# Two attention blocks: first row maxima from the split parts in four banks, the last sums partly on TensorE, and filler matmuls at the start

## The reference

```
block 0, on x[16,128,1024]:
  h = group_norm(x, 32 groups, eps 1e-6) * scale + bias
  q, k, v = Wq^T h + bq, Wk^T h + bk, Wv^T h + bv      # 4 heads of 32 channels
  p = softmax(q^T k / sqrt(128)) over 1024 keys        # per head, 1024 x 1024
  x = (x + Wp^T (v p^T) + bp) / sqrt(2)
block 1, on that x:
  h = group_norm(x, 8 groups, eps 1e-5) * w + b
  q, k, v = qkv_w h + qkv_b                            # one head of 128 channels
  out = proj(softmax(q^T k / sqrt(128)) v) + proj_b + x
```

## Time and profile before

| what | value |
|---|---|
| time before, median of 3 runs | 1682.16 us (1681.73 to 1682.63) |
| the profiled execution's own time | 1681.49 us |
| its span in the profile | 1679.7 us |
| TensorE busy | 1604.5 us, 96% |
| VectorE busy | 1162.1 us, 69% |
| GpSimd busy | 1130.2 us, 67% |
| ScalarE busy | 1069.1 us, 64% |
| first score matmul of round 0 starts at | 66.49 us |
| last matmul of block 0's attention, then the wait for GpSimd's sums, ends at | 1596.62 us |

### The profile page before, as it was taken

One profiled execution on the slowest core, in us unless ns is written; L12 is line 12 of the kernel. 1 busy time (PEld: TensorE's weight loads), 2 busy tenths in 40 slices (PEclk: granted clock), 3 DMA queues, 4 the chain that ended last, 5 costly groups with the idle time before them and its releaser, 6 DMA issues.

```text
span 1679.7 us, 25530 instructions
## 1 busy us (share of the span) xinstructions
PE 1604.5 (96%) x9319; PEld 1067.4 (64%) x9319; DVE 1162.1 (69%) x1961; ACT 1069.1 (64%) x1825; POOL 1130.2 (67%) x535
## 2 busy tenths in 40 slices
PE   3888899999999999999999999999999999999888
PEld 2343466666666666666667666766666676766567
DVE  3677677777777777777777777677777767775342
ACT  1245576766667666766766676767667676767634
POOL 2088787676668867666786767668776766788700
PEclk8599899999999999999999999999999999999989
DMA  6132304041311404141140414113041412200000
GB/s 201 66 76 72 68 13 131 21 126 39 101 45 57 108 20 126 39 117 36 51 107 21 125 39 126 38 64 83 33 114 38 126 38 66 67 20 8 7 7 20
DMA packets 47660, 111.69 MB, mean 66 GB/s; under 512 B 5808, under 2 KB 6448, under 8 KB 47536
## 3 DMA queue, kind: packets, MB, share of 16 engines
q1 hardware_dynamic: 47536, 110.06, 23.5%
HBM read 67.84 MB, written 41.94 MB: 65 GB/s over the span
## 4 chain that ended last, share of the span: by engine, by line
PE 89%; DVE 5%; ACT 3%; DMA 2%; issue 1%; POOL 0%; SPq 0%; ACTq 0%; POOLq 0%
PE bank L899 15%; PE acc L838 14%; PE scores L877 14%; PE scores L820 14%; PE scores L864 7%; PE scores L856 4%; PE acc L904 3%; PE bank L908 3%; PE scores L857 3%; PE scores L858 3%; PE bank L904 3%; DVE halfmax L707 3%; PE bank L922 2%; PE bank L926 2%; ACT turned L569 1%
## 5 line engine op out<-in xcount | busy, mean ns | idle before, releaser
L510 POOL TENSOR_TENSOR sum<-sum,probs 128x1024 f32<-128x1024 f32 x448 | 1049.7, 2379 | 398.2 <-PE acc L838 397.0
L707 DVE TENSOR_REDUCE halfmax<-bank 128x1 f32<-128x512 f32 x1024 | 678.1, 685 | 246.3 <-PE bank L899 242.4
L549 ACT ACTIVATE probs<-scores 128x512 f32<-128x512 f32 x896 | 516.2, 598 | 185.4 <-PE scores L820 181.9
L899 PE MATMUL bank<-k_stack,q_stack 96*128 96x512 f32 x1024 | 445.4, 455 | 29.0 <-DVE halfmax L707 11.1
L820 PE MATMUL scores<-q_stack,k_stack 97*128 97x512 f32 x1024 | 448.6, 455 | 2.3 <-DMA q_stack<-neg 2.2
L899 PEld LDWEIGHTS bank<-k_stack,q_stack 96*128 96x128 f32 x1024 | 196.4, 194 | 162.0 <-DVE halfmax L707 90.6
L877 PEld LDWEIGHTS scores<-v,turned 128*128 128x128 f32 x1952 | 252.3, 191 | 38.5 <-ACT turned L569 19.2
L877 PE MATMUL scores<-v,turned 128*128 128x128 f32 x1952 | 259.5, 276 | 4.3 <-ACT turned L569 3.8
L820 PEld LDWEIGHTS scores<-q_stack,k_stack 97*128 97x128 f32 x1024 | 194.6, 192 | 99.5 <-issue 78.6
L562 ACT ACTIVATE probs<-scores,negmax 128x1024 f32<-128x1024 f32 x128 | 142.7, 1115 | 155.9 <-DVE negmax L746 155.9
L838 PE MATMUL acc<-probs,v 128*32 128x512 f32 x1792 | 222.5, 608 | 0.0
(11 more groups left out here) (86 smaller groups left out, 1293.9 us busy)
## 6 DMA issues: line engine op xcount, KB each, us to landing
q_stack<-parts_dram SPq DMA_DIRECT2D x96, 256.0 KB, 5.2
k_stack<-parts_dram SPq DMA_DIRECT2D x96, 256.0 KB, 7.2
xin<-x_dram SPq DMA_DIRECT2D x16, 512.0 KB, 3.4
x<-x_dram SPq DMA_DIRECT2D x16, 512.0 KB, 3.5
parts_dram<-q_hi SPq DMA_DIRECT2D x16, 512.0 KB, 2.6
parts_dram<-q_lo SPq DMA_DIRECT2D x16, 512.0 KB, 3.1
parts_dram<-k_hi SPq DMA_DIRECT2D x16, 512.0 KB, 3.1
parts_dram<-k_lo SPq DMA_DIRECT2D x16, 512.0 KB, 4.2
```

The lines of the kernel that those rows point to most:

```text
L510: pool.tensor_tensor(total, total, probs[:, ring_slot(i, half, kt), 2 * two:2 * two + 2, :], ALU.add).then_inc(added[two], 1)
L549: act.activation(dst, score_bank(i, index), ACT.Exp).then_inc(exp_done, 1)
L707: dve.tensor_reduce(halfmax[:, h, t, half:half + 1], banks[p][:, :], AX.X, ALU.max).then_inc(bank_free[p][VE], 1)
L899: mm = pe.matmul(dst[:, :], qs[0:SPLIT, q_half(i, arg // FIRST), h, tile(t % 4)], ks[0:SPLIT, i % 2, h, halves(half)], start=True, stop=True)
```

## The change

Start. The constants and the vectors are issued from ScalarE's queue, the weights stay on SP's, and the three loads of `x1` move behind the stacking transfers. The statistics of image 0 come before VectorE's wait for the constants; mean, variance and normalisation are woven into the preparation. ScalarE does a one-column exponential first. GpSimd's memset of 32 partitions of `k_stack` moves behind the first reciprocal root. TensorE multiplies a matrix of ones with a tile of ones six times, once and twice more (`idle`) at three places of the preparation; the products are not used.

First maxima. The head's 32 pieces multiply the parts themselves, three matmuls of 32 partitions each with the head's row group as tile position, and go round four banks: both halves of `scores1` and `bank0`, `bank1`. They no longer wait for the stacks. The statistics, mean and variance of image 1 move from before them to between them (gaps 20, 24, 28).

End. GpSimd leaves out the last two steps (four additions) of the last half of the last image; TensorE adds those exponentials by itself, in the same accumulation of ones. The piece moves from gap 6 to gap 4, its reciprocals from gap 7 to gap 5.

```diff
 HEAD = [
-    ("stats0", 0, 0, None, None, 0), ("mean0", 0, 0, 1, None, 1), ("var0", 0, 0, 2, None, 2),
-    ("affine0", 0, 0, None, None, 3), ("norm0", 0, 0, None, 4, None),
+    ("norm0", 0, 0, None, 4, None),
...
-    ("stats0", 0, 1, None, None, 9), ("mean0", 0, 1, 9, None, 9), ("var0", 0, 1, 10, None, 10),
 ] + [("max", n, 0, 10 + n, None, 10 + n) for n in range(FIRST)] + [
+    ("stats0", 0, 1, None, None, 20), ("mean0", 0, 1, 24, None, 24), ("var0", 0, 1, 28, None, 28),
...
+DIRECT = 2
-    ("save", 1, -1, None, 4, None), ("sums", 1, -1, 6, 6, None), ("recip", (1, 0), -1, None, None, 7),
+    ("save", 1, -1, None, 4, None), ("sums", 1, -1, 4, 4, None), ("recip", (1, 0), -1, None, None, 5),
...
+            shared = (0, 1, 3, 4) if head_maximum(piece) else (0, 1)
...
-        banks = [ps(f"bank{b}", [C, HALF]) for b in range(2)] + [acc]
+        banks = [ps(f"bank{b}", [C, HALF]) for b in range(2)] + [acc, scores1[:, 0:HALF], scores1[:, HALF:N]]
...
             sp.dma_start(xin[:, :], x_dram[0]).then_inc(xin_loaded, 16)
-            sp.dma_start(consts[:, :, :], constants).then_inc(const_loaded, 16)
             sp.dma_start(wts[:, :, :], weights).then_inc(const_loaded, 16)
-            sp.dma_start(vecs[:, :], vectors).then_inc(const_loaded, 16)
-            for i in range(3):
-                sp.dma_start(x1[:, i, :], x_dram[i]).then_inc(x1_loaded, 16)
...
             stack_queries(0, 1)
+            for i in range(3):
+                sp.dma_start(x1[:, i, :], x_dram[i]).then_inc(x1_loaded, 16)
...
+            rstd(0, 0)
+            pool.wait_ge(rstd_done[0], 1)
+            pool.memset(ks[SPLIT:C, :, :, :].bitcast(F32), 1.0).then_inc(prep_pool, 1)
...
-                for n in range(2 * ADDS):
+                for n in range(2 * ADDS - (2 * DIRECT if i == images - 1 else 0)):
...
+            act.dma_start(consts[:, :, :], constants).then_inc(const_loaded, 16)
+            act.dma_start(vecs[:, :], vectors).then_inc(const_loaded, 16)
+            act.wait_ge(prep_pool, 1)
+            act.activation(rowsum[:, 0:1], ones[:, 0:1], ACT.Exp)
...
+                    if head_maximum(piece):
+                        if arg in (0, FIRST // 2):
+                            for part_of in (("q0", 0, 0), ("k0", half, 0)):
+                                pe.wait_ge(bank_free[bank_of(part_of)][VE], given_back(part_of))
+                        for n, (q, k) in enumerate(((0, 2), (0, 3), (1, 2))):
+                            mm = pe.matmul(dst[:, :], part[q][head(h), tile(t)], part[k][head(h), halves(half)],
+                                           start=n == 0, stop=n == 2, tile_position=(DH * h, 0))
...
+                    for kt in (0, *direct):
+                        for h in range(HEADS):
+                            src = probs[:, ring_slot(i, arg, kt), h, :] if kt else sum0[:, arg, h, :]
+                            mm = pe.matmul(dst[head(h), :], ones[:, :], src, start=kt == 0,
+                                           stop=kt == (direct[-1] if direct else 0), tile_position=(0, DH * h))
...
+            def idle(count):
+                for _ in range(count):
+                    pe.matmul(scores[0:DH, 1, :], ones[:, :], probs[:, RING - 1, 0, :], start=True, stop=True)
+            pe.wait_ge(idle_ready, 1)
+            pe.wait_ge(prep_pool, 1)
+            idle(6)
             pe.wait_ge(const_loaded, 48)
+            work(("mean0", 0, 0))
+            idle(1)
...
+            work(("var0", 0, 0))
+            idle(2)
             pe.wait_ge(prep_ve, 6)
```

More of the change, by code:

```diff
@@ L192, in all_pieces, with head_maximum @@
     return out
+def head_maximum(piece):
+    return piece[0] == "max" and piece[2] == 0 and piece[1] < FIRST
+BANKS = 5
+FIRST_PIECES = [(("mean0", 0, 0), -1), (("var0", 0, 0), -1)]
 def bank_uses(images):
     back = {VE: dict(all_pieces(VE, images)), SC: dict(all_pieces(SC, images))}
-    uses, counts, last, free = {}, [[0, 0] for _ in range(3)], [None] * 3, [(-1, 0)] * 3
-    for piece, _ in all_pieces(PE, images):
+    uses, counts, last, free = {}, [[0, 0] for _ in range(BANKS)], [None] * BANKS, [(-1, 0)] * BANKS
+    for piece, _ in FIRST_PIECES + all_pieces(PE, images):
         if piece[0] in BANKED:
-            b = 2 if piece[0] in IN_ACC and piece[1] == 0 else 0 if free[0] <= free[1] else 1
+            shared = (0, 1, 3, 4) if head_maximum(piece) else (0, 1)
+            b = 2 if piece[0] in IN_ACC and piece[1] == 0 else min(shared, key=lambda n: free[n])
             uses[piece] = (b, sum(counts[b]), counts[b][0], counts[b][1], last[b])
             last[b] = BANKED[piece[0]]
-            free[b] = (back[last[b]][piece], len(uses))
+            free[b] = (back[last[b]].get(piece, -1), len(uses))
             counts[b][0 if last[b] == VE else 1] += 1
@@ L308, in bass_two_attention_blocks @@
         prep_pool = sem("prep_pool")
+        idle_ready = sem("idle_ready")
         xin_loaded = sem("xin_loaded")
@@ L311, in bass_two_attention_blocks @@
         x1_formed = sem("x1_formed")
-        bank_full = [sem(f"bank_full{b}") for b in range(3)]
-        bank_free = [{VE: sem(f"bank_free_ve{b}"), SC: sem(f"bank_free_sc{b}")} for b in range(3)]
+        bank_full = [sem(f"bank_full{b}") for b in range(BANKS)]
+        bank_free = [{VE: sem(f"bank_free_ve{b}"), SC: sem(f"bank_free_sc{b}")} for b in range(BANKS)]
         gn_step = [sem(f"gn_step{b}") for b in range(2)]
@@ L597, in high @@
                 if (which, half) == (0, 0) and i and b == 0:
+                    if i == 1:
+                        act.wait_ge(rowmax_done, 1)
                     for stacked in (*stacked_q, *stacked_k):
@@ L759, in output @@
                                          op0=ALU.add, op1=ALU.add).then_inc(bank_free[p][VE], 1)
+            dve.memset(probs[:, RING - 1, 0, :], 1.0).then_inc(idle_ready, 1)
+            half_stats(0, 0, 0)
+            half_stats(0, 1, 0)
             dve.wait_ge(const_loaded, 48)
+            group_mean(0, 0)
             for b in range(2):
@@ L812, in score @@
                 half, kt = divmod(n, KT)
+                if i == 0 and index == 0:
+                    pe.wait_ge(prep_pool, 3)
                 if kt == 0 and h == 0:
@@ L846, in score1 @@
                         pe.wait_ge(bank_free[bank_of(piece)][VE], given_back(piece))
+                    if j == 0:
+                        for n in range(FIRST):
+                            pe.wait_ge(bank_free[bank_of(("max", n, 0))][VE], given_back(("max", n, 0)))
                 T = KT * j + t
@@ L918, in work @@
                 elif name == "sums":
+                    direct = range(KT - DIRECT, KT) if (i, arg) == (images - 1, 1) else ()
                     for two in range(2):
-                        pe.wait_ge(added[two], (KT - 1) * (2 * i + arg + 1))
-                    for h in range(HEADS):
-                        mm = pe.matmul(dst[head(h), :], ones[:, :], sum0[:, arg, h, :], start=True, stop=True,
-                                       tile_position=(0, DH * h))
+                        pe.wait_ge(added[two], (KT - 1) * (2 * i + arg + 1) - len(direct))
+                    for kt in (0, *direct):
[3 more added lines that the diff above has]
+                                           stop=kt == (direct[-1] if direct else 0), tile_position=(0, DH * h))
                 elif name == "proj":
```

11 lines of the change are left out of this document (6 added, 5 removed).

## The result

| | kernel before | changed kernel |
|---|---|---|
| median (lowest to highest) of 4 runs, us | 1682.39 (1681.73 to 1683.42) | 1658.57 (1654.42 to 1659.37) |
| profiled execution, its span, us | 1681.49, 1679.7 | 1654.42, 1652.6 |
| TensorE busy | 96% | 97% |

The ratio is 0.9853 (95%: 0.9836 to 0.9870). 1653.0 (1647 to 1660) was predicted: the time lies in the range, 5.6 us above the forecast. The profiled execution gained 27.1 us; it is also the fastest of the four, and the medians differ by 23.8.

A forecast was written before the change was run, and what follows sets the result against it. TensorE, busy 96%, bounds the middle rounds; gains lie in head and tail. Terms 3.4 + 1.8 + 11.1 + 1.85 = 18.1, with 1.5 and 9.5 29.1 us, take 1681.49 to 1652.4, 1653 on the median's scale; range 1647 to 1660.

The forecast's parts named there:

- start of q: Head, up to image 0's normalisation: it starts at 12.9 against 16.27, minus 3.4 us; bounds plus 3.7 to minus 5.5.
- q, k, v: Head, q, k and v matmuls: 7.0 us instead of 8.8, minus 1.8, if the clock is up; otherwise 0.
- trip through DRAM: Head: first maxima read the parts without waiting for their way to DRAM and back, minus 11.1 us.
- the maxima: Head's 32 maxima: VectorE is the bound with four banks, 23.9 us against 25.75, minus 1.85.
- round 0 and later rounds: Round 0: TensorE may come in warm, between 0 and minus 4 us, taken as minus 1.5.
- tail, from the last mark: End of the kernel: projection 8.6 us earlier, up to 1.9 more if the clock stays up; minus 9.5 taken.
- Rival 1: Start: filler stays slow and delays the mean; 9 us less gain, 1662 us. Chance 0.10.
- rival 2: Maxima: row tiles overlap only with a neighbour, or loads wait; phase 28 to 29, time 1657 to 1658. Chance 0.17.
- rival 3: Maxima: no overlap and a low clock, 41.1 us, so minus 11 in all, 1671. Chance 0.06.
- rival 4: Maxima: each pass waits for its predecessor's end and its own load; plus 70, so 1723 us. Chance 0.03.

The follow-up runs named there:

- more filler, until q: Changed kernel with its own filler plus two more products of ones while ScalarE normalises image 0: 1658.89 us, ratio 0.9857 to the kernel before.
- The repetition: The changed kernel timed and profiled once more with nothing edited: 1658.02 us, ratio 0.9852 to the kernel before; profiled span 1655.8.
- Filler around the shift: Changed kernel without filler at the start, one product of ones before and one behind the transpose of the maxima: 1654.72 us, ratio 0.9832 to the kernel before.

## Why the prediction was right, step by step

| term, us | predicted | measured in the profiled execution |
|---|---|---|
| start of q | -3.4 | -3.0 (17.56 to 14.52) |
| q, k, v | -1.8 | -0.6 |
| trip through DRAM | -11.1 | -11.2 |
| the maxima | -1.85 | -1.65 |
| round 0 and later rounds | -1.5 | +1.0 |
| tail, from the last mark | -9.5 | -11.6 |
| sum | -29.1 | -27.1 |

The table is added up from one profile of each kernel. The forecast came true, in part by luck: q, k and v came out 1.2 us worse than forecast and the rounds 2.5, the tail 2.1 better.

- **Start.** Right in size: six fillers took 6.96 (6.9 predicted), the mean came at 8.40 (8.0) and the normalisation at 13.13 (12.9). But I counted the whole gain as the change's and never asked what the start would be without the filler. There it was 2.64 better. The rest of the edits at the start make the gain (without filler q starts at 11.88, 5.68 earlier than before the change; how much each of them does was not tried), and the filler gives part of it back. Rival 1 had only the dear form of this, a filler that stays slow, and its start was mis-added: 11.3, three products of 1.71, 1.9 and 0.3 are 18.6 and not 20.
- **q, k and v.** "Minus 1.8, if the clock is up": it wasn't. The filler raised it, 1.75 us of standing still lost it. This condition was named, and my own sum had the gap in it. The price itself was near: with the clock up all the way (more filler, until q) the stretch took 7.3, and 7.0 was forecast.
- **Trip through DRAM.** As forecast. Putting it back costs 15 us, but that run also goes back to two banks, so the 15 is not the trip's alone. No stack transfer made the first score late: the transfer engines are done at about 44 us (45 forecast), and the maxima's own transfer takes 1.85 as before.
- **Maxima.** VectorE was the bound in the main, 24.10 us against 23.9. Inside that sum two errors cancel: reductions came 0.60 to 0.61 apart and not 0.645, some 1.3 us less in 32, and VectorE stood 1.4 us for TensorE around the variance of image 1. The reason was right (heads overlap, as the tiles of 32 columns did), the clock of 1.00 wrong, and it didn't matter, since the row above has three passes under way at once. Rivals 2, 3 and 4 are out by the phase's 24.10. With four tiles of one head in a row it took 30.7. Its 1.28 for a maximum is rival 3's mechanism, passes one at a time at the low clock, wherever one head is alone; that the phase lies near rival 2's 28 to 29 says nothing for rival 2. (Rival 2's "plus 4.3" with VectorE's 2.4 exposed is 4.9 by its own terms.) That it was cheap to be wrong on the clock is due to the order of heads and to four banks. The Trainium skill ("TensorE: Matmul & The Clock Gate", Part 3, The mechanism) says that weight loads overlap a running matmul only in another row group; in the changed kernel's timeline

```profile
24.39 0.50 PE L932 MATMUL scores<-k_hi,q_hi 32*128 32x512 f32 x1
24.50 0.18 PEld L932 LDWEIGHTS scores<-k_lo,q_hi 32*128 32x128 f32 x1
```

  a load lies inside a matmul, both of rows of one head's high and low parts. With the predecessor shown in the earlier trace rows, the trace disagrees with that rule twice. The same section of the Trainium skill also lets a load run ahead where it goes to a background weight buffer; if that is what happens here, no run shows it.
- **Round 0.** The failed step. I took minus 1.5 between 0 and minus 4, for a TensorE that comes in warm. It came in at the low level, as before: the clock was 0.50 in the maxima and stayed there until 59 us, and the first 23.0 us of the round were as long as in the kernel before. So the term's own mechanism gave 0. Then the clock fell again at 73, and the stretch of 7.68 us shown above took 10.56. That is 2.9 of the 3.0 by which the first half round grew (42.80 between marks instead of 39.80). By the fourth mark most of it had come back. From first to fourth mark the kernels of this study needed 127.3 to 133.4 us, the kernel before 129.7; the size of this term is thus chance of a few microseconds, and my range for it should have had both signs.
- **Tail.** The path was right to 0.1: the projection was forecast 8.6 earlier and came 8.5 earlier. What comes behind it was mis-sized: up to 1.9 was forecast, and it was 3.1 in the first execution, where the projection was at the high level (1.10), and 1.6 in the second, where it was at the low one (2.04). So the tail is 11.6 or 10.1, inside the 8.6 to 10.5 only the second time. The eleven profiles with this tail fall into the same two kinds: last mark to end is 126.0 to 126.1 in the four where the projection took 1.10, and 127.3 to 128.1 in the seven where it took 1.87 to 2.05. The level there goes with 1.2 to 2.1 us, and one and the same program had it either way.
- **Profiled against timed.** The rest of the miss is that the profiled execution of the changed kernel was 4.2 below its median, while I carried the two over with only the 0.67 of the kernel before between them. The repetition shows where such differences arise.

**Open.** Why the granted clock falls at 73 in the changed kernel, in a stream that ran at 1.00 in the kernel before, isn't settled. TensorE was busy 3.32 of the 4 us before the fall, and much the same, 7.61 of 9.00, from 86 to 95 in the kernel before, where the clock held. No run here separates what the engine did in the head from the time at which it did it. Filler around the shift and an earlier head did not move the time.

## What to carry to other kernels

A detour through DRAM that only lays data out for taller tiles can be skipped for the first use: quarter-height tiles from the small parts did it, on condition that neighbours in the queue use different rows and that there are enough banks for the consumer to be the bound; without the first condition the head's 16.45 us shrank by 6.7, without the second by all. Filler to warm TensorE stands in its queue, so compare its end with the arrival of the input behind it, and ask whether the engine stands still again before the work that it is for; here the kernel without it was 3.1 us faster, and 1.5 of that stands at the first score. Read a change at the end of a program from a mark close to it: the projection's start gave 8.5 in every profile, while the time moved by 2 us with the clock. Price a gain of under two microseconds in front of long rounds with a term of both signs: five kernels without filler, whose first marks differ by 1.0, were timed at 1654.7 to 1655.6.

## What of the hardware was not expected

- The granted clock fell to 0.50 at about 28.6 us with TensorE in unbroken work on 32-row tiles since 25 us. With four tiles of one head in a row it fell at about 27 and stayed there, with 6.00 of 6.00 us busy from 34 to 40. In round 0 it stayed at 0.50 with 9.00 of 9.00 busy (73 to 82). Being busy doesn't by itself hold or bring back the upper level.
- The granted clock of the rows doesn't show a slow start. In the changed kernel it reads 1.00 up to 15.0 us, while the first four passes of the filler stand 0.86 apart and the later ones 0.43. The kernel before has 1.00 at 18 to 20 us, where its q products take 2.08 and 1.71. There the level must be read from durations.
- Matmuls of different 32-row tiles run side by side, three starting within 0.21 us, and make up for the low clock. Passes of one head follow each other at 0.43.
